# Output projection of the first batch placed inside the state-space loop, and u computed a chunk ahead

## The chip, the cores and the metric

The kernel runs on one core of one Trainium2 chip. The metric is the device time of one execution in microseconds (us); lower is better. The engines of the core work side by side and wait for one another by semaphores: TensorE (PE in the profile, its weight loads PEld), VectorE (DVE), ScalarE (ACT), GpSimd (POOL) and SyncE (SP), which here only issues DMA transfers.

## What is computed

One decoder block for a batch of 2 sequences with 512 rows and 1024 columns: a state-space mixer, a quantised product with a context matrix, and a quantised feed-forward part, each added to x. The change touches the mixer and the start of the second part. The mixer of one batch row (D = 2048, N = 16):

```python
proj = hidden_states @ W_in.T
u, gate = jnp.split(proj, 2, axis=-1)
u = jax.nn.silu(causal_conv(u, conv_w) + conv_b)          # 4 taps
dt, Bm, Cm = jnp.split(u @ Wx.T, [R, R + N], axis=-1)     # each then _rmsnorm
delta = jax.nn.softplus(dt @ Wdt.T + dt_bias)
def step(state, xs):                                      # over the 512 rows
    state = jnp.exp(d_t[..., None] * A) * state + (d_t * u_t)[..., None] * B_t[:, None, :]
    y_t = jnp.einsum('bdn,bn->bd', state, C_t)
y = (ys + u * D_param) * jax.nn.silu(gate)
return y @ W_out.T                                        # the output projection
```

(`causal_conv` stands for the reference's convolution call.)

## The kernel before, in words

The program is three functions one after the other, each of which ends when all its engines are done: `mixer`, `attend` (the context product) and `feed_forward`.

**The loop of the mixer.** The 2048 channels are cut in 16 chunks of 128, the chunks in 4 groups of 4 (GD = 4). With two batches that makes 8 groups G = 0 to 7; 0 to 3 are the first batch, 4 to 7 (GROUPS = 4 and up) the second. In each group the 16 states are 16 steps n, so there are 128 steps s = 16 G + n. In a step ScalarE computes four decays (`decay`), GpSimd four products with B (`times_b`), and VectorE runs four scans over time (`scan`, j = 0 to 3), one for each chunk. TensorE turns the scanned states of the step (`turn_state`, 16 transposes in four parts t = 0 to 3), which it can start when the fourth scan is done, so its step n lies beside step n+1 of VectorE. VectorE adds three of the four turned parts to `acc` (`add_states`) between its next scans, ScalarE and GpSimd the fourth. A VectorE instruction of step n+1 waits for TensorE if TensorE is late by more than a scan.

**Work laid beside the steps.** Every engine's program is written out by hand in one order, and functions of G and n say what stands in which step: on TensorE, between the parts t, the products of the second batch's u (`u_part`, 8 products of 128x512 in f32 for a chunk, during G = 0 to 3), those of the gate of each group (`gate_part`, 32 for a group, range given by `gate_range`), the product that gives dt, B and C (`ssm_product`), `dt_product`, the way back of y (`turn_y`, in n = 0 to 3 of the next group) and the output projection (`wout_part`: 2 products for each of 16 chunks c of a tile of 128 rows, weights through `p_ring`). ScalarE copies the gate out of PSUM (`gate_copy`), applies silu to it at the end of n = 0 of the next group (`silu_gate`: table load, silu over 128x2048, table load), starts the convolution of a finished chunk of u (`conv_first`), whose other three taps are VectorE's (`conv_rest`). The PSUM banks are shared: `bank_u` and `bank_s` hold u, the gate or the projection by turns.

**The output projection.** Its input y is known only after a group's last step, goes to memory (`yT_dram`) and comes back turned. There are 8 tiles of 128 rows, 4 for each batch. Tiles 0 to 2 are done beside groups 5 to 7 (WOUT_BESIDE = 3, 32 products each), tile 3 after the last step (`wout_last`: half of its chunks before the last `turn_y`, half behind it). The second batch's tiles 4 to 7 are done in `attend` (`project`), beside its stages.

**`attend`.** STAGES is a pipeline over the 8 tiles: in stage i VectorE adds the projection to x for tile i (`stage_a`), codes tile i-1 (`stage_b`), finishes tile i-2 (`stage_c`) and tile i-3 (`stage_d`); TensorE first does the share of `project` that BESIDE gives to the stage, then turns tile i-1's codes, and multiplies them with the context (`cross`). `cross(i)` waits until `stage_c` of the tile before has read the banks. Tiles under FIRST take their projection from memory (`attn_dram`), the others from `bank_o`.

## Time and profile before

| What | Value |
|---|---|
| runs without profile | 1631.77 us median of 3 (1631.59 to 1633.46) |
| profiled execution | 1635.13 us, its span 1633.3 us |
| mean granted TensorE clock | 0.950 |
| busy over the span | PE 1386.8 us (85%), DVE 1318.5 (81%), ACT 932.5 (57%), POOL 930.4 (57%) |
| scans of the loop | first at 181.7 us, last ends at 1133.5 us |
| `attend` | first instruction at 1181.1 us; `feed_forward`'s first product at 1378.2 us |

All times below are of the profiled execution. A window row of the trace gives, for each engine, its busy time in a stretch; where the busy time of one engine fills the stretch, that engine is the candidate for the bound, and the waits named in square brackets at an instruction say who was waited for.

### The profile page before, as it was taken

To read this page: it belongs to the slowest core of one execution; us is meant where nothing else is said; L and a number is where in the kernel's file an instruction comes from. 1 tells how busy PE (TensorE), PEld (TensorE's weight loads), DVE (VectorE), ACT (ScalarE), POOL (GpSimd) and SP (SyncE) were. 2 spreads that over 40 slices of the span, in tenths; PEclk is the share of its full clock that TensorE was granted. 3 is DMA by queue.
4 is the path that set the end of the run, shared out by engine and by line. 5 is a ranking of instruction groups with operands and counts; after the bars stand their busy time and mean duration, and the time that the engine had idled before them with its cause. 6 is when DMAs were issued, how large, how long until landed. Compare 5 with 4: busy or idle time off the path is not lost. (4 is left out here: it accounts for less than half of the span.)

```text
span 1633.3 us, 17931 instructions
## 1 busy us (share of the span) xinstructions
PE 1386.8 (85%) x5550; PEld 724.3 (44%) x5576; DVE 1318.5 (81%) x1641; ACT 932.5 (57%) x1375; POOL 930.4 (57%) x767
## 2 busy tenths in 40 slices
PE   6998677788888887768898898888899985999798
PEld 3443243444444453444454554544444442444443
DVE  6586899999999889999999999898068465777684
ACT  1212467768767756877778778765143222567570
POOL 0000497898898868899989999896101000334200
PEclk9999798999999998987999999999999996999899
DMA  8598243453452432344574782772482104679404
GB/s 281 173 348 303 71 142 110 153 168 110 147 163 102 164 106 98 112 146 149 209 247 143 258 277 98 273 225 114 172 330 78 52 26 134 126 186 204 99 11 169
DMA packets 155468, 264.38 MB, mean 162 GB/s; under 512 B 76560, under 2 KB 94096, under 8 KB 149552
## 3 DMA queue, kind: packets, MB, share of 16 engines
q1 hardware_dynamic: 151056, 236.27, 44.7%
q10 hardware_dynamic: 4320, 27.00, 4.6%
q8 instruction: 43, 0.70, 0.2%
q14 instruction: 49, 0.40, 0.1%
HBM read 207.60 MB, written 38.60 MB: 151 GB/s over the span
## 5 line engine op out<-in xcount | busy, mean ns | idle before, releaser
L1144 DVE TENSOR_TENSOR_SCAN hbuf<-decay,hbuf 128x512 f32<-128x512 f32 x502 | 598.2, 1211 | 21.0 <-ACT decay L823 20.6
L823 ACT ACTIVATE decay<-delta,chan_sb 128x512 f32<-128x512 f32 x502 | 343.8, 687 | 226.5 <-DVE hbuf L1144 223.7
L629 PE MATMUL turn<-ident,hbuf 128*128 128x128 f32 x2048 | 327.1, 289 | 165.5 <-DVE hbuf L1144 139.8
L629 PEld LDWEIGHTS turn<-ident,hbuf 128*128 128x128 f32 x2048 | 252.5, 148 | 423.2 <-DVE hbuf L1144 217.9
L1158 DVE SCALAR_TENSOR_TENSOR acc<-turn,pn,acc 128x512 f32<-128x512 f32 x360 | 262.9, 730 | 25.5 <-PE turn L629 24.3
L978 POOL TENSOR_TENSOR hbuf<-wout,sx 128x512 f32<-128x512 f32 x172 | 213.5, 1272 | 15.0 <-DVE wout L1131 15.0
L978 POOL TENSOR_TENSOR hbuf<-du,sx 128x512 f32<-128x512 f32 x172 | 213.3, 1276 | 0.0
L999 POOL TENSOR_TENSOR acc<-acc,part 128x512 f32<-128x512 f32 x120 | 153.0, 1275 | 21.9 <-ACT part L833 21.9
L1847 PE MATMUL bank<-codes,wout 128*128 128x512 bf16 (+1 forms) x690 | 153.3, 382 | 1.7 <-PEq L1261 1.0
L611 PE MATMUL bank_g<-wout,codes 128*128 128x512 f32 x256 | 135.6, 616 | 0.0
L541 PE MATMUL bank_u<-wout 128*128 128x512 f32 x224 | 112.4, 621 | 3.4 <-DMA wout<-in_wu 2.5
L1551 POOL TENSOR_TENSOR rstd<-rstd,mhalf 128x1 f32<-128x1 f32 x16 | 12.9, 808 | 176.2 <-DVE rstd L1590 176.2
L1847 PEld LDWEIGHTS bank<-codes,wout 128*128 128x128 bf16 (+1 forms) x704 | 69.5, 99 | 85.3 <-issue 4.2
L978 POOL TENSOR_TENSOR hbuf<-du,b_more 128x512 f32<-128x512 f32 x84 | 104.6, 1278 | 0.0
L978 POOL TENSOR_TENSOR hbuf<-wout,b_more 128x512 f32<-128x512 f32 x84 | 104.4, 1275 | 0.0
L541 PE MATMUL bank_s<-wout 128*128 128x512 f32 x208 | 102.3, 607 | 0.0
L611 PE MATMUL bank_s<-wout,codes 128*128 128x512 f32 x192 | 98.3, 594 | 0.0
L1022 POOL TENSOR_TENSOR rs<-rs,mhalf 128x12 f32<-128x12 f32 x2 | 4.5, 2275 | 144.6 <-DVE rs L1107 144.6
L833 ACT ACTIVATE part<-turn,pn 128x512 f32<-128x512 f32 x120 | 80.5, 671 | 7.2 <-PE turn L629 7.1
L1006 POOL TENSOR_TENSOR y_out<-y_out,gbuf 128x512 f32<-128x512 f32 x32 | 40.8, 1274 | 69.8 <-ACT y_out L848 69.8
L1969 POOL TENSOR_TENSOR hid<-gs,wout 128x512 f32<-128x512 f32 (+1 forms) x29 | 37.0, 1275 | 70.4 <-DVE wout L2005 68.4
L765 ACT ACTIVATE wout<-wout,rnd,row_scales 128x512 f32<-128x512 f32 (+1 forms) x88 | 70.4, 800 | 0.0
(219 smaller groups left out, 2130.8 us busy)
## 6 DMA issues: line engine op xcount, KB each, us to landing
wout<-in_woutT SPq DMA_DIRECT2D x48, 512.0 KB, 4.8
sx<-bt_scratch SPq DMA_DIRECT2D x86, 256.0 KB, 3.7
codes<-in_wg SPq DMA_DIRECT2D x8, 2048.0 KB, 9.9
ubuf<-u_scratch SPq DMA_DIRECT2D x16, 1024.0 KB, 7.0
wout<-in_w_gate SPq DMA_DIRECT2D x26, 512.0 KB, 4.9
wout<-in_w_up SPq DMA_DIRECT2D x26, 512.0 KB, 4.9
raw_d<-in_w_down ACTq DMA_DIRECT2D x8, 1376.0 KB, 7.2
b_more<-bt_scratch SPq DMA_DIRECT2D x42, 256.0 KB, 3.6
```

The costliest lines, as they stand in the source:

```text
L541: last = pe.matmul(u_bank(i)[:, :], w_ring[:, i % 2, k * P:k * P + P], xT[:, k, b * L:b * L + L], start=(k == 0), stop=(k == KC - 1))
L611: mm = pe.matmul(gate_bank(G, j)[:, :], wg_buf[:, k, j * P:j * P + P], xT[:, k, b * L:b * L + L], start=(k == 0), stop=(k == KC - 1))
L629: last = pe.transpose(turn[t % 2][:, j * P:j * P + P], hbuf[:, s % 4, j, t * P:t * P + P], ident[:, :])
L765: act.activation(v, v, ACT.Identity, bias=rnd[0:n, 0:1], scale=keep.iw[0:n, u % 2, c:c + 1])\
L823: act.activation(decay_place(q), delta[:, G % 2, j, :], ACT.Exp, scale=a_col(GD * (G % GROUPS) + j, n)).then_inc(dA_done, 1)
L833: act.activation(part[:, k % 2, :], turn[ZT % 2][:, :], ACT.Copy, scale=pn[:, G // GROUPS, ZT, c:c + 1]).then_inc(part_done, 1)
L978: pool.tensor_tensor(hbuf[:, s % 4, j, :], du[G % 2][:, j, :], b_row[s % 3], ALU.mult).then_inc(dbu_done, 1)
L999: pool.tensor_tensor(a, a, part[:, k % 2, :], ALU.add).then_inc(part_added, 1)
L1006: pool.tensor_tensor(y, y, gbuf[:, j, :], ALU.mult).then_inc(y_done, 1)
L1144: dve.tensor_tensor_scan(h, decay_place(q), h, 0.0, ALU.mult, ALU.add).then_inc(scan_done, 1)
L1158: dve.scalar_tensor_tensor(a, state, pn[:, G // GROUPS, t, c:c + 1], a, ALU.mult, ALU.add)\
L1847: last = pe.matmul(banks(c, b)[0:r, :], wT[:, c % WT, m, k, 0:r], keep.codes[:, k, b * L:b * L + L], start=(k == 0), stop=(k == KC - 1))
```

## The change

It moves work between places in the written order, and changes no arithmetic. The core of the diff:

```diff
-        WOUT_BESIDE = GROUPS - 1
+        WOUT_BESIDE = GROUPS
+        P_FIRST = (2, 3, 2, 3, 3, 3)
+        def p_products(s):
+            G, n = s // N, s % N
+            if G == GROUPS and 9 <= n < 9 + len(P_FIRST):
+                return P_FIRST[n - 9]
+            return 2 if G > GROUPS and n < KC else 0
...
+        def u_products(s):
+            G, n = s // N, s % N
+            if G >= GROUPS:
+                return 0
+            if G == GROUPS - 1:
+                return 6 if n < 4 else 0
+            return 4 if n < (8 if G == 0 else 6) or n >= 14 else 0
...
         def gate_range(G, n):
-            lo, per = (9, 3) if G == 0 else (5, 3) if G == GROUPS - 1 else (8, 4)
+            lo, per = (6, 4) if 1 <= G < GROUPS else (1, 4) if G == GROUPS else (8, 4)
...
         def gate_copies(G, n):
-            at = (-1, -1, 14, 16) if G == 0 else (9, 12, 14, 16) if G == GROUPS - 1 else (12, 14, 15, 16)
+            at = (-1, -1, 12, 14) if G == 0 else (9, 12, 14, 15) if G == GROUPS - 1 else (10, 12, 14, 15) if G < GROUPS else (4, 6, 8, 10) if G == GROUPS else (12, 14, 15, 16)
...
+        SSM_AT = (10, 12)
...
-            return 5 if G == GROUPS - 1 else 9 if G < GROUPS - 1 else None
+            return 5 if G == GROUPS - 1 else (9, 7, 7)[G] if G < GROUPS - 1 else None
...
-            return q % GD == 2 and (n == 1 and G >= 1 or n == 10 and G < GROUPS - 1)
+            if j == 3:
+                return n == 1 and G == GROUPS
+            return j == 2 and (n == 1 and G >= 1 or G < GROUPS - 1 and n == silu_u_step(G) + 1)
...
-            wout_last(KC, DC)
+            wout_last(KC, 3 * GD)
             for j in range(GD):
                 turn_y(NG - 1, j)
             wout_last(0, KC)
+            wout_last(3 * GD, DC)
...
+                    if not early_decay(GD * s + 3):
+                        decay(s, 3)
                     if n == 0 and G >= 1:
                         for j in gate_copies(G - 1, N):
                             gate_copy(G - 1, j)
-                    decay(s, 3)
...
-                    if b == 1 and g >= 1 and n == 9:
-                        wout_copy(g - 1)
+                    if G > GROUPS and n == 9:
+                        wout_copy(g)
+                    if G == GROUPS + 1 and n == 0:
+                        wout_copy(0)
...
-    FIRST = TT
+    FIRST = TT + 1
-    BESIDE = [[((TT, TT + 1), DC // 4 * i, DC // 4 * (i + 1))] for i in range(4)]
-    BESIDE += [[((TT + 2,), 0, 8)], [((TT + 2,), 8, DC), ((TT + 3,), 0, 2)], [((TT + 3,), 2, 9)], [((TT + 3,), 9, DC)]]
+    BESIDE = [[((FIRST,), 0, 8)], [((FIRST,), 8, DC)]] + [[((FIRST + 1,), 4 * i, 4 * i + 4)] for i in range(4)]
+    BESIDE[5] += [((FIRST + 2,), 0, 2)]
+    BESIDE += [[((FIRST + 2,), 2, 9)], [((FIRST + 2,), 9, DC)]]
```

In words. All four tiles of the first batch are projected in the loop: tile 0 beside steps 9 to 14 of group 4, tiles 1 to 3 beside groups 5 to 7; group 4's gate moves up to steps 1 to 8 to make room. Tile 4, the second batch's first, takes the place behind the last step: its chunks 8 to 11 before the last `turn_y`, chunks 0 to 7 behind it, and last chunks 12 to 15, which come from the last group and are stored and loaded in between (`load_yT_last(1)`). `attend` projects three tiles (5, 6, 7). The second batch's u is computed a chunk ahead: one chunk of the next group already in steps 14 and 15, so that its `conv_first` stands at the end of step 0 of the next group. `ssm_product` of groups 0 to 2 is split in two halves, in steps 10 and 12, and gets a bank of its own (`ssm_bank`); its sum `add_ssm` moves from step 15 to 14. The gates of groups 1 to 3 end in step 13 and their last copy moves from step 0 of the next group to step 15 (14 for group 0). In groups 6 and 7 it stays in step 0, but behind `decay(s, 3)`. One semaphore (`ms_done`) goes and `yT_keep` comes.

TensorE's order in `attend`, stages 2 and 3 (a row is a run of equal instructions; `bank_o` is `project`, `bank_t` the turning of codes, `bank_p<-ctx_q,codeT` is `cross`). Before:

```order
L1418 MATMUL bank_o<-wout,codes 128x512 x16
L1433 MATMUL bank_t<-identb,code 128x128 x8
L1450 MATMUL bank_b<-ones,codeT 128x1 x8
L1461 MATMUL bank_p<-ctx_q,codeT 128x512 x16
L1418 MATMUL bank_o<-wout,codes 128x512 x16
L1433 MATMUL bank_t<-identb,code 128x128 x8
```

And now:

```order
L1483 MATMUL bank_o<-wout,yT 128x512 x8
L1498 MATMUL bank_t<-identb,code 128x128 x8
L1515 MATMUL bank_b<-ones,codeT 128x1 x8
L1526 MATMUL bank_p<-ctx_q,codeT 128x512 x16
L1483 MATMUL bank_o<-wout,yT 128x512 x8
L1498 MATMUL bank_t<-identb,code 128x128 x8
```

The share of `project` ahead of each `cross` is halved in stages 2, 3 and 4, and in stage 5 it goes from 20 products to 12; in stages 0, 1, 6 and 7 it is as long as before. (A product of the order is two instructions in the trace.)

ScalarE's order at the head of a group (steps 0 and 1 of group 2; `gbuf<-bank_s` is the gate copy, `gbuf<-gbuf` the silu, `wout<-bank_u` is `conv_first`). Before:

```order
L765 ACTIVATE wout<-wout,rnd,row_scales 128x512
L854 ACTIVATE gbuf<-bank_s 128x512
L823 ACTIVATE decay<-delta,chan_sb 128x512 x2
L833 ACTIVATE part<-turn,pn 128x512
L823 ACTIVATE decay<-delta,chan_sb 128x512
L823 ACTIVATE bank_g<-delta,chan_sb 128x512
L858 ACT_TABLE_LOAD
L858 ACTIVATE gbuf<-gbuf 128x2048
L859 ACT_TABLE_LOAD
L823 ACTIVATE decay<-delta,chan_sb 128x512 x3
```

And now:

```order
L818 ACTIVATE wout<-wout,rnd,row_scales 128x512
L878 ACTIVATE decay<-delta,chan_sb 128x512 x2
L888 ACTIVATE part<-turn,pn 128x512
L878 ACTIVATE decay<-delta,chan_sb 128x512
L878 ACTIVATE bank_g<-delta,chan_sb 128x512
L913 ACT_TABLE_LOAD
L913 ACTIVATE gbuf<-gbuf 128x2048
L914 ACT_TABLE_LOAD
L797 ACTIVATE wout<-bank_u,chan_sb 128x512
L801 DMA wout<-in_wu 128x1024
L878 ACTIVATE decay<-delta,chan_sb 128x512 x3
```

The gate copy ahead of the decays is gone from here, and a `conv_first` stands between the silu and the next decays. VectorE's `conv_rest` for it is in step 1, after the second scan.

TensorE's order in steps 10 and 11 of group 4 (`turn` is `turn_state`; the other rows are the gate before and `wout_part` now). Before:

```order
L588 MATMUL bank_m<-ssm,wdt_sb 128x512
L629 MATMUL turn<-ident,hbuf 128x128 x4
L611 MATMUL bank_s<-wout,codes 128x512
L629 MATMUL turn<-ident,hbuf 128x128 x4
L611 MATMUL bank_s<-wout,codes 128x512
```

And now:

```order
L634 MATMUL bank_m<-ssm,wdt_sb 128x512
L675 MATMUL turn<-ident,hbuf 128x128 x8
L706 MATMUL bank_u<-wout 128x512
L706 MATMUL bank_s<-wout 128x512
L675 MATMUL turn<-ident,hbuf 128x128 x4
L706 MATMUL bank_u<-wout 128x512
L706 MATMUL bank_s<-wout 128x512
L675 MATMUL turn<-ident,hbuf 128x128 x4
```

The first row is step 9's `dt_product`; the parts t of a step that have no product between them run together (x8). Step 10 holds six products of the projection (three chunks, the third behind the last row here) where it held four of the gate; step 11 holds four.

## Rows read from the trace of the kernel before

Columns of a window row: from:to, length, busy us (and instructions) of PE, PEld, DVE, ACT and POOL, granted TensorE clock (share of full speed), share of the DMA engines, GB/s.

**Rows 1.** Windows: groups 1, 3, 4, 5, the mixer's end, `attend`:

```profile
307.40:428.60 121.20, 101.95 (x432) 57.55 (x432) 116.27 (x131) 92.34 (x140) 107.61 (x88) 0.96 0.43 145
...
551.40:690.50 139.10, 111.48 (x452) 61.55 (x452) 124.25 (x143) 94.23 (x142) 107.42 (x87) 0.93 0.35 119
690.50:801.20 110.70, 85.43 (x364) 51.43 (x364) 106.66 (x118) 85.68 (x133) 106.71 (x88) 0.85 0.42 138
801.20:912.80 111.60, 99.16 (x432) 55.31 (x432) 106.77 (x118) 86.92 (x136) 106.21 (x87) 1.00 0.63 215
...
1133.50:1181.10 47.60, 40.91 (x128) 20.39 (x128) 2.25 (x3) 10.40 (x15) 6.54 (x6) 0.99 0.45 166
1181.10:1343.00 161.90, 152.83 (x553) 71.57 (x561) 100.13 (x175) 49.28 (x54) 10.71 (x17) 0.98 0.34 124
```

**Rows 2.** The same view for one stage of `attend`:

```profile
1259.10:1279.30 20.20, 18.99 (x76) 9.04 (x75) 12.51 (x23) 4.73 (x6) 1.10 (x2) 1.00 0.15 52
```

**Rows 3.** TensorE in `attend`, in order of time (start us, us):

```profile
1236.80 3.40 PE L1461 MATMUL bank_p<-ctx_q,codeT 128*128 128x512 bf16 x15
...
1255.92 3.40 PE L1461 MATMUL bank_p<-ctx_q,codeT 128*128 128x512 bf16 x15
...
1260.06 13.97 PE L1418 MATMUL bank_o<-wout,yT 128*128 128x512 f32 x32
...
1276.03 1.67 PE L1461 MATMUL bank_p<-ctx_q,codeT 128*128 128x512 bf16 x7
```

**Rows 4.** VectorE in `attend`, in order of time:

```profile
1231.12 0.75 DVE L1633 SCALAR_TENSOR_TENSOR xr<-fix,sc,xr 128x512 f32<-128x512 f32 x1
...
1238.18 0.69 DVE L1577 TENSOR_SCALAR ctx_raw<-ctx_raw 128x1024 f32<-128x1024 f32 x1 [4.55 <-ACT ctx_raw L1496]
...
1243.50 0.81 DVE L1610 TENSOR_SCALAR xn<-xr,mv,rstd 128x1024 f32<-128x1024 f32 x1
...
1253.07 0.75 DVE L1633 SCALAR_TENSOR_TENSOR xr<-fix,sc,xr 128x512 f32<-128x512 f32 x1
...
1268.12 0.75 DVE L1633 SCALAR_TENSOR_TENSOR xr<-fix,sc,xr 128x512 f32<-128x512 f32 x1
```

**Rows 5.** ScalarE, then VectorE, at step 0 of group 2:

```profile
434.19 0.60 ACT L854 ACTIVATE gbuf<-bank_s 128x512 f32<-128x512 f32 x1 [2.72 <-PE bank_s L611]
...
442.50 1.30 ACT L823 ACTIVATE decay<-delta,chan_sb 128x512 f32<-128x512 f32 x2
...
435.40 2.34 DVE L1144 TENSOR_TENSOR_SCAN hbuf<-decay,hbuf 128x512 f32<-128x512 f32 x2 [1.41 <-ACT decay L823]
```

**Rows 6.** VectorE: a `conv_rest`, and the wait in step 15 behind `ssm_product`:

```profile
379.47 2.31 DVE L1077 SCALAR_TENSOR_TENSOR wout<-bank_s,chan_sb,wout 128x511 f32<-128x511 f32 x3
...
422.67 0.75 DVE L1158 SCALAR_TENSOR_TENSOR acc<-turn,pn,acc 128x512 f32<-128x512 f32 x1 [1.23 <-PE turn L629]
```

**Rows 7.** Windows: group 1 step 1; group 3 steps 1-6, step 4; group 4 step 6:

```profile
313.87:322.33 8.46, 8.32 (x34) 5.18 (x35) 7.38 (x9) 7.60 (x8) 7.48 (x7) 0.82 0.53 216
...
559.30:620.20 60.90, 54.72 (x214) 31.29 (x214) 49.35 (x57) 37.59 (x51) 41.11 (x34) 0.92 0.42 145
...
590.40:600.80 10.40, 10.40 (x43) 5.93 (x42) 8.83 (x12) 5.92 (x9) 7.46 (x7) 1.00 0.16 50
...
733.00:739.40 6.40, 5.65 (x18) 3.31 (x18) 6.40 (x8) 4.74 (x7) 6.40 (x7) 0.53 0.60 199
```

**Rows 8.** TensorE in a step that follows an idle time, group 1:

```profile
368.13 1.12 PE L629 MATMUL turn<-ident,hbuf 128*128 128x128 f32 x4 [3.25 <-DVE hbuf L1144]
...
372.43 0.60 PE L629 MATMUL turn<-ident,hbuf 128*128 128x128 f32 x4
...
375.12 1.12 PE L588 MATMUL bank_m<-ssm,wdt_sb 64*128 64x512 f32 x2
```

**Rows 9.** The mixer's end: GpSimd's last gated y, and SyncE's issues:

```profile
1164.23 1.26 POOL L1006 TENSOR_TENSOR y_out<-y_out,gbuf 128x512 f32<-128x512 f32 x1 [1.44 <-ACT y_out L848]
...
1167.85 0.81 SPq L501 DMA_DIRECT2D codes<-yT_scratch  x2
```

More of the change, by code:

```diff
@@ L218, in u_count @@
             return Gu + 1 + (Gu >= GROUPS - 1)
-        RELU_STEP = 9
+        MS_STEP = (7, 21)
+        RELU_STEP = 10
         def unit_rows(u):
@@ L712, in _ @@
                         turn_y(G - 1, n)
-                    if G < GROUPS - 1 and n == 13 or G == GROUPS - 1 and n == 5:
+                    if G < GROUPS - 1 and n in SSM_AT:
+                        ssm_product(GROUPS + g, 2 * SSM_AT.index(n), 2 * SSM_AT.index(n) + 2)
+                    if G == GROUPS - 1 and n == 5:
                         ssm_product(GROUPS + g)
@@ L937, in _ @@
                         decay(s + 1, 1)
-                        if early_decay(GD * (s + 1) + 2):
-                            decay(s + 1, 2)
+                        for j in range(2, GD):
+                            if early_decay(GD * (s + 1) + j):
+                                decay(s + 1, j)
                     if paired:
@@ L1384, in _ @@
             load_attn(2)
+            load_yT(1)
             load_yT(2)
-            load_yT(3)
             load_x(3)
```

195 lines of the change are left out of this document (114 added, 81 removed).

## The prediction

> **What bounds the kernel now.** I read the windows by stretch first. In the loop VectorE is the full engine: 116.3 of 121.2 us in group 1, 106.7 of 110.7 in group 4 [rows 1]. A step in which nothing goes wrong takes 6.4 us, all of it VectorE (last of [rows 7]). So work laid beside a step on TensorE is free as long as TensorE is done in time, and a step gets longer either by VectorE's own work (a `conv_rest` is 2.31 us, 2.23 with the overlap [rows 6]) or by a wait of VectorE. In `attend` it is the other way round: TensorE is busy 152.8 of 161.9 us, VectorE 100.1 [rows 1], and in one stage of 20.2 us TensorE has 19.0 and VectorE 12.5 [rows 2]. Of such a stage `project` is 13.97 us for 32 instructions [rows 3], so 0.44 us for one and 0.87 us for a product of the order.
>
> The Trainium skill speaks against me here. It says (Trainium Kernel Development and Optimization, Performance Expectations) that matmul busy time is a bad metric, because matmuls are pipelined; if the 152.8 us were only overlapping ends, nothing would come of taking products out. But the 32 instructions stand in 13.97 us from first start to last end, 0.44 us apart at full clock, with no wait named. So I count the trace's spacing; by the skill's doubt this part would be worth 0.
>
> **attend: minus 20.** The change takes one tile of four out: 16 instructions (8 products) in each of stages 2 to 5, 16 x 0.437 = 7.0 us a stage, 28 in all. I follow which wait comes last then.
> Stage 2: `cross` starts at 1236.80 [rows 3]. TensorE would be there at 1229.8, but it must wait for `stage_c` of the tile before, which ends at 1231.12 + 0.75 = 1231.9 [rows 4]. Gain 4.9.
> Stage 3: VectorE waited for ScalarE's context pieces until 1238.18 [rows 4], and ScalarE for TensorE. Now it is free of stage 2's work at 1233.6, so the pieces (5.3 us, 1238.18 to 1243.50) end at about 1239.0, 4.5 earlier. From 1243.50 to the end of `stage_c` at 1253.07 + 0.75 are 10.3 us of VectorE, so the next `cross` can start at 1249.3 instead of 1255.92. Gain so far 6.6.
> Stage 4: VectorE needed 1268.87 - 1253.82 = 15.1 us to the next end of `stage_c`, 2.2 of it waits for ScalarE that goes with TensorE: 12.9, so 1262.2. TensorE's way is 20.1 (1276.03 - 1255.92) - 7.0 = 13.1, so 1262.4. Gain 13.6.
> Stage 5: 12 products left, TensorE bound again: another 7.0, 20.6. Stages 6 and 7 are as long as before and TensorE bound, and the tail behind them moves along. I take **20.3**. Bounds: 28 if VectorE gives way, 13 if stages 4 and 5 each lose half.
>
> **The mixer's end: 0.** TensorE has 40.9 of 47.6 us there [rows 1], 32 products before and now. What is new is that the last 4 chunks wait for y of group 7 to be stored and loaded. 4 chunks fewer stand ahead of the last `turn_y`, so all of y is 8 x 0.87 = 6.9 us earlier: GpSimd ends at 1165.5 - 6.9 = 1158.6, the stores have landed at 1167.85 - 6.9 = 1161.0 [rows 9]. The load of 256 KB then has the 6.9 + 2.3 us until TensorE has done chunks 0 to 7. A transfer would have to take over 9 us to be seen.
>
> **Step 0 of a group: minus 7.7.** ScalarE's gate copy waits for TensorE until 434.19 and stands ahead of `decay(s, 3)`, so the fourth scan waits 1.41 [rows 5]; groups 2, 3, 5, 6 and 7 have this 1.41, group 4 has 1.05. The copy moves to step 15 for groups 2 to 5: 1.5 + 1.5 + 1.15 + 1.5 with the overlap that the wait breaks. In groups 6 and 7 the copy stays but behind the decay: it then delays the next decay by some 0.5, gain 1.0 each.
>
> **A conv at step 1: plus 2.3, and a cold TensorE: plus 3.** Step 1 takes 8.46 us, since ScalarE is in the table loads and the silu (first of [rows 7]). One would hope that the conv of the chunk ahead fills this hole. It doesn't: `conv_first` stands behind the silu, where the decays resume at 442.50, 6.0 us after the step's first scan at 436.5 [rows 5]. With its 0.7 us the conv can begin at 6.7 and VectorE sits in front of it from 4.4; then 2.2 of conv, scan, add, scan: the step ends at 11.9 instead of 8.46. That is 3.4 for a conv that cost 2.2 elsewhere: +1.2 in each of groups 1 and 2 (group 3 below). While VectorE waits TensorE is idle for about 4 us. After 3.25 idle, two sets of transposes and two products take 372.43 - 368.13 = 4.3 us instead of 375.12 - 372.43 = 2.7 [rows 8], at half clock. TensorE's step 1 holds 4 products and `turn_y`, some 7.1 us, 8.7 with this; VectorE's step 2 lasts 6.4 and forgives 0.6 more, so step 3 waits 1.5: +3.0 for two groups. Bounds for both terms together: 0 and 9.
>
> **Groups 0 to 2, rest: minus 5.** `ssm_product` in one piece (8 instructions, 3.5 us) makes step 15 wait 1.23 in groups 1 and 2 and 0.86 in group 0 [rows 6]. Halves of 1.7 beside 4 gate products make 7.1 us of TensorE, within what a step forgives: -3.4 (the broken overlap included; -1 if the halves wait as well). With silu of u at step 7, step 8, which waited for a cold TensorE, and step 10, which waited for the silu, become one: -0.9 twice.
>
> **Group 3: minus 4.** Steps 1 to 4 carried 8 products of u, and TensorE fills them: 10.40 of 10.40 us at full clock (third of [rows 7]). Steps 1 to 6 took 60.9 us (second of [rows 7]). With 6 products such a step is 10.4 - 1.7 = 8.7, the same as VectorE with a conv (6.4 + 2.2). Step 1 becomes 11.9, step 2 6.4, step 3 8.7 + 3.4 of lateness from step 2's 8.7 + 1.6 cold, then 8.8, 8.8 and the silu's 9.4: 57.4. -3.5 here; its step 0 is counted above. The wait of chunk 15 for the conv of chunk 13 falls in this lateness. With what the earlier end of the gates spares I take **-4**.
>
> **Group 4: 0.** 32 products more, 27.8 us, on a TensorE with 85.4 of 110.7 busy [rows 1]. Step 1: `decay(s, 3)` now goes ahead of the silu, -1.1. Waits in steps 5 to 9 cost 2.2 (110.7 less 16 x 6.43, 4 x 0.6 of `delta_add`, and 3.2 in steps 0 and 1), and they come from TensorE at half clock: 0.53 in step 6, where it has only transposes [rows 7]. The gate at steps 1 to 8 keeps the clock up: -2.2. Against it: six products and the transposes are 7.1 to 7.4 us, over 6.43, in steps 10, 12, 13 and 14, a third of which VectorE feels, +1; the first chunk waits at step 9 for a gate copy that ScalarE makes in step 10, +1.2; steps 14 and 15 of group 3 have only transposes now, so the group starts at half clock, +1.
> The Trainium skill (TensorE: Matmul & The Clock Gate, Part 4: PE-mode transpose) says that PE-mode transposes do not count as busy for the clock; the rows agree (0.53 with only transposes, 1.00 in group 5, where products are mixed in [rows 1]). If products so mixed did not count either, the rule would cost this change dearly, which is the rival below.
> Groups 5 to 7 hold what they held. `load_yT(1)` can only start when tile 0 is done, at step 15; if it is late, step 1 has slack.
>
> **Sum.** -20.3 (attend), 0, -7.7, +5.3, -5.2, -4, -0.1: -32.0. Against the profiled execution of 1635.1 (span 1633.3) that is 1603.1; that execution is 3.4 above the median without profile, so against 1631.77: **1599.8**.
>
> **Rivals.**
> (a) The chain in `attend` does not go at TensorE's pace once a tile is out: ScalarE's in-order copies and `stage_c` take turns, and stages 2 to 5 give 8 to 10 instead of 20. For it: VectorE's 12.9 and TensorE's 13.1 leave nothing over, and stage 3 is already lost. Against: ScalarE has 4.7 us in a stage of 20 [rows 2]. 1611.
> (b) The loop gives nothing: the conv behind the silu costs its upper bound 9, and the ssm halves wait too. 1611 to 1613. For it: TensorE's slack in group 1 is only 19 us [rows 1].
> (c) More than I count: `conv_first` costs little, group 4 gains 3: 1593.
> (d) Slower: mixed with transposes the projection's products are not enough to keep the clock, and group 4 runs at half clock throughout. Then its 64 products take 1.74 instead of 0.87, the transposes 3.8 instead of 1.9 a step, the group some 180 us instead of 110: 1670. It decides once seven of its 16 steps run so (4 to 5 us each against the 32). Against it: group 5 has the same mix at clock 1.00 [rows 1].
> (e) No change: products in `attend` are hidden anyway, and the loop breaks even.
>
> **How the numbers follow.** Forecast 0.70, (a) 0.10, (b) 0.11, (c) 0.06, (d) 0.02, (e) 0.01. The range reaches to (c) below and to (a) above, 1592 to 1611. A measurement of this kernel tells 0.2%, 3.3 us, from no change: faster in all cases but (d) and (e), 0.97, same 0.01, slower 0.02.
>
> **What would show it.** Right: `cross` to `cross` some 13 us in stages 3 and 4, `attend` 20 us shorter; the fourth scan of step 0 waits no more in groups 2 to 5; step 1 of groups 1 to 3 takes 11 to 12 us with VectorE's wait in front of `conv_rest`; steps 2 to 5 of group 3 under 9.5 us but one; the last 4 chunks of tile 4 start without a wait. Wrong: TensorE's clock at half in steps 9 to 14 of group 4, VectorE waiting there for TensorE by more than 1 us a step, or stages of 16 us and more in `attend`.

## The result, and the profile after

| | before | after |
|---|---|---|
| runs | 1632.62 us median of 4 | 1621.62 us median of 4 (1621.10 to 1627.92) |
| ratio | | 0.9932, 95% interval 0.9904 to 0.9961 |
| profiled execution, its span | 1635.13, 1633.3 | 1627.92, 1626.0 |
| start to the first scan | 181.7 | 178.6 |
| the loop, first scan to last | 951.8 | 957.1 |
| last scan to the first product of `attend` | 47.7 | 47.5 |
| `attend`, first product to the first of feed-forward | 197.0 | 178.8 |
| feed-forward to the end | 255.1 | 264.0 |

About 11 us faster where 32 were forecast; the range (1592 to 1611) doesn't hold it. The first and the last part of the table are untouched by the change and vary from one execution to the next: the start took 177.7 to 181.7 us and feed-forward 254.2 to 267.4 in the twelve traces of this case. The three parts between give 5.3 - 0.2 - 18.2 = -13.1. So `attend` did nearly what was forecast (-20.3) and the loop did not: +5.3 where the steps add up to -11.7.

The windows of after that answer to [rows 1]: groups 1, 3, 4 and 5, the mixer's end, `attend`.

```profile
306.00:428.10 122.10, 103.77 (x441) 58.16 (x440) 116.05 (x131) 92.83 (x141) 106.49 (x87) 0.97 0.42 139
550.60:688.00 137.40, 109.27 (x440) 61.94 (x440) 124.08 (x142) 94.05 (x143) 108.49 (x87) 0.89 0.39 133
688.00:801.60 113.60, 103.78 (x431) 60.20 (x432) 107.11 (x118) 85.76 (x134) 108.10 (x89) 0.92 0.58 189
801.60:916.80 115.20, 99.89 (x426) 56.10 (x424) 106.87 (x118) 87.45 (x137) 104.95 (x86) 0.96 0.68 235
1135.60:1183.10 47.50, 40.92 (x128) 20.39 (x128) 2.27 (x4) 10.40 (x15) 6.57 (x6) 1.00 0.43 149
1183.10:1327.20 144.10, 126.48 (x489) 59.30 (x497) 99.78 (x174) 49.32 (x54) 12.89 (x17) 0.96 0.39 143
```

VectorE's busy time is what it was (107.1 us in group 4 for 106.7, 106.9 in group 5 for 106.8): what the loop lost is waits of VectorE. In `attend` TensorE has 26.4 us less work and the stretch is 17.8 shorter.

Group by group, from the first scan of one to the first scan of the next, with my forecast put together from the prediction's terms, and the control, which is a second trace of the same kernel:

| group | before | after | change | forecast | control |
|---|---|---|---|---|---|
| 0 | 125.74 | 127.42 | +1.7 | -0.9 | 127.80 |
| 1 | 121.16 | 122.15 | +1.0 | +0.6 | 122.09 |
| 2 | 122.80 | 122.36 | -0.4 | -1.0 | 122.37 |
| 3 | 139.06 | 137.39 | -1.7 | -5.5 | 137.33 |
| 4 | 110.76 | 113.57 | +2.8 | -1.3 | 113.56 |
| 5 | 111.60 | 115.23 | +3.6 | -1.5 | 113.36 |
| 6 | 111.38 | 110.92 | -0.5 | -1.0 | 110.77 |
| 7 | 109.28 | 108.02 | -1.3 | -1.0 | 108.00 |

Groups 3, 4 and 5 miss by 13 us together. I went there step by step (a step runs from its first scan to the next step's) and looked at what VectorE waits for. Four places of after, in order of time; each row has start, length, engine, line, operation, and in brackets the idle time ahead of it and who ended it.

```profile
315.14 1.91 ACT L913 ACTIVATE gbuf<-gbuf 128x2048 f32<-128x2048 f32 x1
...
318.36 0.78 ACT L797 ACTIVATE wout<-bank_u,chan_sb 128x512 f32<-128x512 f32 x1
...
319.17 2.32 DVE L1136 SCALAR_TENSOR_TENSOR wout<-bank_u,chan_sb,wout 128x511 f32<-128x511 f32 x3 [3.16 <-ACT wout L797]
...
631.15 1.06 PE L675 MATMUL turn<-ident,hbuf 128*128 128x128 f32 x4 [3.46 <-DVE hbuf L1204]
632.01 1.92 PE L657 MATMUL bank_u<-wout,codes 128*128 128x512 f32 x2
...
634.81 0.75 DVE L1218 SCALAR_TENSOR_TENSOR acc<-turn,pn,acc 128x512 f32<-128x512 f32 x1 [0.68 <-PE turn L675]
...
759.78 0.58 ACT L909 ACTIVATE gbuf<-bank_s 128x512 f32<-128x512 f32 x1
...
760.57 1.66 PE L706 MATMUL bank_u<-wout 128*128 128x512 f32 x2 [3.19 <-issue]
...
764.69 0.75 DVE L1218 SCALAR_TENSOR_TENSOR acc<-turn,pn,acc 128x512 f32<-128x512 f32 x1 [3.20 <-PE turn L675]
...
803.35 0.60 SPq L447 DMA_DIRECT2D wout<-yT_scratch  x1
...
812.80 2.04 PE L706 MATMUL bank_u<-wout 128*128 128x512 f32 x2 [2.81 <-issue]
...
817.44 0.75 DVE L1215 TENSOR_SCALAR acc<-turn,pn 128x512 f32<-128x512 f32 x1 [4.47 <-PE turn L675]
...
822.63 0.75 DVE L1218 SCALAR_TENSOR_TENSOR acc<-turn,pn,acc 128x512 f32<-128x512 f32 x1 [1.53 <-PE turn L675]
```

- **315 to 319, step 1 of group 1** (groups 2 and 3 alike): `conv_first` stands behind the silu and its table load, VectorE waits 3.16. The step takes 12.55, forecast 11.9.
- **631 to 635, steps 8 and 9 of group 3**: TensorE comes back from 3.46 idle at half clock (a product 1.92 instead of 1.02), with four gate products to do where it had three. VectorE waits here (0.68) and twice more (0.68 and 1.62); steps 9 to 11 take 12.77, 7.42 and 8.15 instead of 11.55, 6.63 and 7.73.
- **760 to 765, step 10 of group 4**: the first product of tile 0 starts 0.2 after the gate copy's end at 760.36. TensorE stood 3.19 for it, with the step's transposes behind it, and VectorE stood 3.20 for those.
- **803 to 823, steps 0 to 2 of group 5**: `load_yT(1)` is issued at 803.35, 1.9 after the group's first scan; the first product of tile 1 starts 9.45 later, at half clock, again ahead of the transposes. VectorE waits 4.47 and 1.53.

The last two are one pattern: an instruction of TensorE that waits for something else, with `turn_state` behind it in the order, which VectorE needs.

`attend` after, TensorE in order of time, answering to [rows 3]; start, length:

```profile
1234.27 3.40 PE L1526 MATMUL bank_p<-ctx_q,codeT 128*128 128x512 bf16 x15 [1.11 <-DVE xr L1698]
...
1251.37 1.01 PE L1526 MATMUL bank_p<-ctx_q,codeT 128*128 128x512 bf16 x2 [3.30 <-DVE xr L1698]
1252.60 4.61 PE L1526 MATMUL bank_p<-ctx_q,codeT 128*128 128x512 bf16 x13 [0.22 <-issue]
...
1257.77 7.03 PE L1483 MATMUL bank_o<-wout,yT 128*128 128x512 f32 x16
...
1267.12 3.40 PE L1526 MATMUL bank_p<-ctx_q,codeT 128*128 128x512 bf16 x15 [0.41 <-DVE xr L1698]
```

`project` is 7.03 us a stage where it was 13.97: the 7.0 of the forecast. In stage 3 TensorE waits 3.30 for VectorE and then does `cross` at half clock (5.84 from first start to last end instead of 3.40). The `cross` of stage 2 stands behind 1.11 of idle time here and keeps full clock; in the control it took 5.09 behind the same 1.11.

### The profile page after: what moved, and what is told of

The parts are those of the page before. It is cut to its first block and busy times, and to the rows that moved or that the text cites. A ratio compares the mean times of both kernels' runs of the same rounds, so it can differ in the third digit from the quotient of the medians.

```text
span 1626.0 us, 17958 instructions
## 1 busy us (share of the span) xinstructions
PE 1383.0 (85%) x5550; PEld 722.4 (44%) x5576; DVE 1318.0 (81%) x1640; ACT 934.2 (57%) x1377; POOL 932.4 (57%) x767
## 5 line engine op out<-in xcount | busy, mean ns | idle before, releaser
L583 PE MATMUL bank_u<-wout 128*128 128x512 f32 x224 | 112.4, 617 | 2.5 <-DMA wout<-in_wu 1.7
L888 ACT ACTIVATE part<-turn,pn 128x512 f32<-128x512 f32 x120 | 80.5, 671 | 13.4 <-PE turn L675 13.3
L706 PE MATMUL bank_u<-wout 128*128 128x512 f32 x128 | 67.7, 611 | 6.0 <-issue 6.0
```

The lines of the kernel that those rows point to most:

```text
L583: last = pe.matmul(u_bank(i)[:, :], w_ring[:, i % 2, k * P:k * P + P], xT[:, k, b * L:b * L + L], start=(k == 0), stop=(k == KC - 1))
L706: last = pe.matmul(bank[:, :], yT_view[c], p_ring[q % 4][:, half * 512:half * 512 + 512], start=(c == 0), stop=(c == DC - 1))
L888: act.activation(part[:, k % 2, :], turn[ZT % 2][:, :], ACT.Copy, scale=pn[:, G // GROUPS, ZT, c:c + 1]).then_inc(part_done, 1)
```

## The experiments

Each edit is measured against the kernel before. The intervals reach 0.2 to 0.4% to either side, 3 to 6 us, as wide as most of the effects; so a kernel's time says whether the whole adds up, and the verdict on a step is read from its trace against the control's. "Loop" is first scan to last scan.

| run | median us | ratio to before, 95% | loop |
|---|---|---|---|
| control | 1622.02 | 0.9919 (0.9895 to 0.9942) | 955.27 |
| conv_first ahead | 1609.91 | 0.9836 (0.9813 to 0.9860) | 944.24 |
| tile 1 later | 1617.47 | 0.9895 (0.9872 to 0.9918) | 955.10 |
| load_wg later | 1624.94 | 0.9927 (0.9903 to 0.9951) | 959.49 |
| group 4's gate earlier | 1617.25 | 0.9897 (0.9875 to 0.9919) | 954.40 |
| attend cut otherwise | 1619.94 | 0.9913 (0.9888 to 0.9937) | 957.06 |
| ssm in one piece | 1625.77 | 0.9953 (0.9934 to 0.9972) | 961.63 |
| group 3's gate thinner | 1621.66 | 0.9913 (0.9888 to 0.9939) | 953.59 |
| before, decay first | 1629.31 | 0.9967 (0.9938 to 0.9996) | 949.63 |
| four together | 1600.57 | 0.9791 (0.9754 to 0.9828) | 937.38 |

**The control**, the changed kernel unedited.

> The changed kernel again, unedited, beside the kernel before, as the measure for the other runs of this chip. Expected: 0.9932 of the kernel before within 0.002, step 1 of the sixth group (group 5) 11.7 us and of groups 1 to 3 12.5 us as in its first trace. If the 11.7 us were an accident of one execution, it would be near 8.5 here.

0.9919: the first ratio again within its error. Step 1 of group 5 took 10.81 and step 2 7.24 (11.66 and 8.09 in the first trace), so the loss there is no accident of one execution, but its size varies by 1.7 us. `attend` took 177.6. By this trace the change is +3.5 in the loop and -19.4 in `attend`.

**conv_first ahead of the silu.**

```diff
+                    c = u_chunk_ready(s)
+                    if n == 0 and c is not None:
+                        conv_first(DC + c)
+                        load_w_after(DC + c)
                     if n == 0 and G >= 1:
                         silu_gate(G - 1)
                     quant(s, 1)
-                    c = u_chunk_ready(s)
-                    if c is not None:
+                    if c is not None and n > 0:
```

> The changed kernel, with the first part of the conv at step 0 of groups 1 to 3 issued by ScalarE ahead of the silu of the gate and not behind it. Theory: step 1 of these groups takes 12.5 us because VectorE stands 3.15 us in front of conv_rest for a ScalarE that is still in the silu, and step 3 is then late by 0.9 to 2.2 because TensorE comes back cold. Then step 1 falls to about 9.2 us (its 8.5 plus what of the conv's 2.2 doesn't fit in the hole), VectorE's wait there is gone, step 3 loses its wait, and the kernel gets 10 to 12 us faster than the changed one: about 1610 us, 0.986 of before. Rival: ScalarE itself is what is full there, and the conv ahead of the silu only pushes the decays of step 1 back by its 0.7 us and the wait moves from conv_rest to the scans; then the gain is under 3 us. Second rival: the cold TensorE is not due to that wait, and step 3 keeps its 1 to 2 us while step 1 gets shorter: 7 us.

Step 1 of group 1 in its trace, ScalarE and VectorE:

```profile
315.68 0.76 ACT L797 ACTIVATE wout<-bank_u,chan_sb 128x512 f32<-128x512 f32 x1
...
317.85 2.31 DVE L1139 SCALAR_TENSOR_TENSOR wout<-bank_u,chan_sb,wout 128x511 f32<-128x511 f32 x3
...
320.97 1.30 ACT L878 ACTIVATE decay<-delta,chan_sb 128x512 f32<-128x512 f32 x2
```

`conv_rest` has no wait in front of it any more. It fills the time in which VectorE would have stood for the decays, which resume 6.7 us into the step (6.0 in the kernel before, where no conv was there; 6.6 in the control). Step 1 takes 9.30 in groups 1 to 3 (12.54 in the control) and step 3 is down to 8.66 in groups 1 and 2 (9.64 and 9.81) and 9.97 in group 3 (10.97). Loop -11.0, ratio -0.0083: the first theory in place and size; the two rivals are out. The wait of step 3 in groups 1 and 2 went together with VectorE's wait in step 1, as the theory of TensorE's cold start (at half clock behind idle time) has it. Steps 1 to 3 of the three groups give 13.7, and steps 6 and 7 of groups 1 and 2 take 2.4 of it back.

**Tile 1 a step later.**

```diff
+            if G == GROUPS + 1:
+                return (0, 2, 2, 2, 2, 2, 3, 3)[n] if n < KC else 0
```

> The changed kernel, with no products of the output projection in step 0 of group 5 and 2,2,2,2,2,3,3 in steps 1 to 7, where it has 2 in each of steps 0 to 7. Theory: load_yT(1) can only be issued at the end of group 4, lands some 9 us later, and TensorE stands in front of the first product with turn_y behind it, on which VectorE's add waits (4.5 us in step 1 and 1.5 in step 2). Then step 1 is 7.3 to 8.5 us instead of 11.7, step 2 6.5 to 7.2 instead of 8.1, nothing is lost in steps 6 and 7 (3 products there beside transposes, at most 0.5 each), and the kernel is 4 to 5 us faster than the changed one, 0.990 to 0.991 of before. Rival: the wait is TensorE's clock after its idle stretch, not the load; then step 1 keeps 10 us or more.

Issue of the load, and the first product of tile 1:

```profile
802.75 0.60 SPq L449 DMA_DIRECT2D wout<-yT_scratch  x1
...
816.72 1.02 PE L708 MATMUL bank_u<-wout 128*128 128x512 f32 x2
```

The product starts without a wait and at full clock, steps 1 and 2 take 8.46 and 6.45: -3.1 against the control, -4.8 against the first trace. So the wait was the load. But the three products in steps 6 and 7 were no "0.5 at most": steps 8 and 9 take 7.50 and 8.75 instead of 7.03 and 6.46, with a wait of 2.18 for TensorE. Group 5 as a whole is 112.97 for 113.36. The control is the shortest of the seven traces in which this group stands as in the changed kernel (113.36 to 115.30, steps 1 and 2 together 18.1 to 19.8 us, 14.9 here), so the edit is worth 0.4 to 2.3 us. The place was right; 2.8 us of the gain were given back in steps 8 and 9 by a TensorE that was behind.

**The gate's weights two steps later.**

```diff
-                    if n == 1 and G >= 1 and G != GROUPS:
+                    if n == (3 if G == GROUPS + 1 else 1) and G >= 1 and G != GROUPS:
                         load_wg(G)
```

> The changed kernel, with the load of the gate's weights (2 MB) for group 5 issued two steps later, behind load_yT(1) and the other loads of step 1. Two theories of the late load. If it is late because 2 MB share the DMA engines with it, its time from issue to landing falls from about 9 us to 4 or 5, step 1 of group 5 is 8 to 9 us instead of 11.7, and the kernel gains 3 us. If it is late because it starts late (at the end of group 4, when tile 0 is done) and its own transfer takes those 9 us, step 1 stays at 11 us or more and the kernel is unchanged within 1 us.

```profile
806.22 0.60 SPq L447 DMA_DIRECT2D wout<-yT_scratch  x1
...
815.69 2.04 PE L706 MATMUL bank_u<-wout 128*128 128x512 f32 x2 [2.82 <-issue]
```

9.47 us from issue to the product, as in after (9.45) and the control (9.43): the 2 MB beside it are not what makes it late. Steps 1 and 2 took 11.68 and 8.08, as in the first trace; step 4 got 2.5 longer: ScalarE's copy of a turned y waits 4.05 us there for the store of the y before it (1.62 in after), and that store was issued at 838.05, with the 2 MB, now issued at 832.36, under way beside it. Below, the DMA view of this kernel from 806 to 816 (busy tenths and GB/s of the engines in slices of 0.25 us, the sum, the loads with size and us from issue to landing), then that of the kernel before from 798 to 810 (slices of 0.3), where the load is issued at 799.90, 1.3 ahead of the group's first scan.

```profile
DMA  7989979899899999999999999999999999999966
GB/s 311 459 360 492 410 328 492 360 426 459 344 492 377 426 426 377 426 393 402 418 369 418 393 377 401 401 385 393 385 393 393 410 410 410 442 434 369 385 270 262
...
q1 hardware_dynamic: 1510, 3.97, 100.5%
...
wout<-yT_scratch SPq DMA_DIRECT2D x1, 1024.0 KB, 9.4
```

```profile
DMA  9820000045655578999999999999999999999979
...
wout<-yT_scratch SPq DMA_DIRECT2D x1, 1024.0 KB, 6.3
```

So the load starts 3.2 us later within the group than before and takes 3.1 longer. It starts later because it is written to wait for the last product of tile 0, which ends at 805.27 here. That it takes longer because the 16 DMA engines are full I infer from this view: 3.97 MB pass in the 10 us, 1 MB of it this load, while before they stood idle when it was issued. What fills them without the 2 MB was issued just ahead, above all three pieces of 512 KB for `load_p` (800.99 to 805.6 here) and u's 1 MB (799.25), and 1 MB right behind. No run took any of these away, so this part of the cause is argued and not shown. The Trainium skill (DMA: Bandwidth & Descriptors, Where 436 GB/s comes from) gives 435 GB/s as the ceiling of the SBUF ports, and the 397 GB/s of this trace stay under it. It puts transfers between HBM and SBUF, which these are, at about 358 a core; the trace lies above that, and the measurement decides.

**Group 4's gate a step earlier.**

```diff
+            if G == GROUPS:
+                at = [0, 0, 4, 8, 12, 17, 22, 27, 32]
+                return at[min(n, 8)], at[min(n + 1, 8)]
...
-(4, 6, 8, 10) if G == GROUPS
+(4, 6, 8, 9) if G == GROUPS
```

> The changed kernel, with group 4's gate products given out as 4,4,4,5,5,5,5 in steps 1 to 7 (4 in each of steps 1 to 8 before) and its last gate copy made in step 9, not 10. Theory: step 10 of group 4 takes 10.35 us because the projection's first chunk stands on TensorE behind ScalarE's gate copy, with the transposes for VectorE's add behind it (wait 3.2). Then step 10 falls to 7.1 or less and steps 11 and 12 to 7.0, at the price of at most 0.3 us in each of steps 4 to 7: 3 to 4 us in all, about 0.990 of before. Rival: it is TensorE's work of that step (products and transposes) and not the copy; then step 10 stays above 9 us.

Step 10 takes 7.03 (10.34 in the control), step 11 7.22 (7.34), step 7 6.99 (6.43): group 4 is 2.9 shorter. It was the copy. But group 5 took 115.30 for 113.36:

```profile
802.62 0.60 SPq L450 DMA_DIRECT2D wout<-yT_scratch  x1
...
812.32 2.04 PE L709 MATMUL bank_u<-wout 128*128 128x512 f32 x2 [2.72 <-issue]
```

Its first scan is at 799.92, so the load is issued 2.7 behind it (after: 1.9; control: 1.9), 9.70 to the product. Whether the wait for tile 1 took part of what the copy's wait gave back is not shown: the first trace of the changed kernel had 115.23 without the edit.

**attend cut otherwise.**

```diff
-        + [[((FIRST + 1,), 4 * i, 4 * i + 4)] for i in range(4)]
+        + [[((FIRST + 1,), lo, hi)] for lo, hi in ((0, 5), (5, 11), (11, 15), (15, DC))]
```

> The changed kernel, with tile 6 of the second batch's projection cut as 5, 6, 4 and 1 products over attend's stages 2 to 5, not 4 in each. Theory: in stages 2 and 3 TensorE stands idle for 1.1 to 3.3 us in front of cross, and after the longest of these it does cross at half clock (5.84 us instead of 2.9); a product of the order put there fills the gap and keeps the clock. Then cross to cross in stage 3 is 13 us where it was 15.7 to 17.1, the stages from 2 to 5 together are 4 to 6 us shorter, and the kernel 0.990 of before. Rival: VectorE and ScalarE set the pace of stages 2 and 3 whatever TensorE does, the clock included; then attend gains less than 1.5 us (only what stage 5 is spared).

```profile
1252.92 3.61 PE L1527 MATMUL bank_p<-ctx_q,codeT 128*128 128x512 bf16 x16 [1.47 <-DVE xr L1699]
...
1266.23 3.61 PE L1527 MATMUL bank_p<-ctx_q,codeT 128*128 128x512 bf16 x16 [0.19 <-DVE xr L1699]
...
1279.55 6.40 PE L1508 MATMUL bank_p<-ctx_q,ones 128*128 128x512 bf16 x16 [3.38 <-DVE xr L1699]
```

The idle time in front of the `cross` at 1252.92 fell from 3.23 (control) to 1.47 and it kept full clock; from it to the next are 13.3 us for 15.2. But from the `cross` before it there are 17.3 for 17.1, since VectorE has no gap between the two in either trace, and the idle time came back in stage 5 (3.38, then 16 instructions at half clock in 6.40): that stage is 21.3 for 19.9. `attend` took 178.0 for 177.6. The rival holds: VectorE sets stages 2 to 5 together now, and a product moved among them moves TensorE's idle time with it. (The 2.9 us that the expectation gives for a `cross` at full clock is 3.40 in the rows.)

**ssm_product in one piece.**

```diff
-                    if G < GROUPS - 1 and n in SSM_AT:
-                        ssm_product(GROUPS + g, 2 * SSM_AT.index(n), 2 * SSM_AT.index(n) + 2)
+                    if G < GROUPS - 1 and n == 12:
+                        ssm_product(GROUPS + g)
```

> The changed kernel, with ssm_product of groups 0 to 2 in one piece at step 12 instead of halves in steps 10 and 12. The prediction counted 3.4 us for taking the piece apart. If that is what the halves are good for, the one piece makes VectorE wait about 1.2 us in step 13 of each of groups 0 to 2, and the kernel gets 2.5 to 3.5 us slower than the changed one. If the gain is only that the product no longer stands at step 14 beside the next u's products, place and not size, it is the same within 1 us. In group 0, where the halves make steps 12 and 14 of 7.25 and 7.6 us, one piece may even be better by 0.5.

Group 1, the product on TensorE and the wait behind it:

```profile
413.65 3.60 PE L608 MATMUL bank_u<-wout,wx_buf 128*96 128x512 f32 x8
...
417.73 0.75 DVE L1218 SCALAR_TENSOR_TENSOR acc<-turn,pn,acc 128x512 f32<-128x512 f32 x1 [1.83 <-PE turn L675]
```

The wait came in step 14 (414.71 to 424.25), not 13, and was 1.83. Group 1 is 1.6 longer than the control's, group 2 3.7 (1.5 of it here, the rest in waits for TensorE at other steps), the ratio 0.0034 higher, with intervals that just overlap: by the trace the halves do work, and it is size, not only place. Group 0 took 127.15 for 127.80 and 127.42: nothing lost by one piece there.

**Group 3's gate thinner.**

```diff
+            if G == GROUPS - 1:
+                at = [0, 4, 7, 10, 13, 17, 21, 25, 29, 32]
+                return at[min(max(n - 6, 0), 9)], at[min(max(n - 5, 0), 9)]
```

> The changed kernel, with group 3's gate products given out as 4,3,3,3,4,4,4,4,3 in steps 6 to 14 instead of 4 in each of 6 to 13. Theory: steps 9 to 11 of group 3 (12.77, 7.42 and 8.15 us; 11.55, 6.63 and 7.73 before the change) are long by 2.4 because four gate products, not three, stand beside the norm and the turns on a TensorE that comes back cold from 3.5 us idle. Then these three steps give back 1.5 to 2.4 us and nothing is lost in 12 to 14: 0.991 of before. Rival: what makes them long is the order of ScalarE's and VectorE's work for the norm (MS at step 7), not TensorE's products; then steps 9 to 11 stay within 0.5 us.

Steps 9 to 11 take 11.54, 6.63 and 8.71: 26.9 for 28.3 in the control, just under the theory's 1.5 to 2.4, and nothing lost in 12 to 14. In two traces with the gate unthinned ("tile 1 later", "ssm in one piece") the three steps take 27.8, so the edit is worth 0.9 to 1.4 there. The other half of what it brings came where I hadn't looked. Windows of group 3's step 15 and group 4's steps 0 to 2, first of the control, then of this kernel (last but two: granted clock):

```profile
684.09:690.52 6.43, 3.42 (x16) 2.28 (x16) 6.43 (x8) 5.63 (x10) 6.43 (x6) 0.58 0.98 415
690.52:697.16 6.64, 4.19 (x16) 3.00 (x16) 6.55 (x9) 4.64 (x7) 6.64 (x7) 0.50 0.71 221
697.16:704.45 7.29, 6.47 (x21) 4.27 (x22) 7.19 (x10) 7.12 (x8) 7.29 (x7) 0.50 0.40 142
704.45:711.63 7.18, 7.18 (x33) 4.71 (x33) 6.56 (x8) 4.51 (x7) 4.55 (x4) 0.92 0.10 37
```

```profile
680.35:686.78 6.43, 4.79 (x22) 2.51 (x22) 6.43 (x9) 5.03 (x10) 6.43 (x6) 1.00 0.11 23
686.78:693.24 6.46, 2.46 (x16) 1.68 (x16) 6.46 (x9) 5.02 (x8) 6.46 (x6) 0.99 0.90 364
693.24:700.53 7.29, 5.81 (x29) 4.33 (x30) 7.19 (x10) 7.12 (x8) 7.10 (x7) 0.77 0.96 337
700.53:706.99 6.46, 6.46 (x32) 3.74 (x30) 6.46 (x9) 4.51 (x7) 4.99 (x5) 1.00 0.39 128
```

In the control TensorE has nothing but the 16 transposes in step 15 and step 0, runs them at 0.58 and 0.50, the 1.2 GHz level, and comes into step 1 at 0.50; 33 instructions then fill all of step 2 and VectorE waits in steps 2 to 5. With three more gate products, written in step 14 and run in step 15 (22 instructions in the first row for 16), step 0 is granted 0.99, step 1 0.77, and steps 2 and 3 take 6.46 and 6.43 instead of 7.18 and 6.95. Group 4 is 1.5 shorter, group 3 1.4. The loop is only 1.7 shorter than the control's, since group 5 took 114.96, within what it takes without an edit.

**The kernel before, with decay first.**

```diff
-                    if n == 0 and G >= 1:
-                        for j in gate_copies(G - 1, N):
-                            gate_copy(G - 1, j)
...
                     decay(s, 3)
+                    if n == 0 and G >= 1:
+                        for j in gate_copies(G - 1, N):
+                            gate_copy(G - 1, j)
```

> The kernel before, with one piece of the change alone: in step 0 of groups 1 to 7 ScalarE makes decay(s, 3) ahead of the gate copy of the group before, not behind it. Theory (the prediction's -1.0 where the copy stays in step 0): the wait of 1.4 us in front of the fourth scan goes, the next decay is delayed by some 0.5, so step 0 of groups 2, 3, 5, 6 and 7 is 0.8 to 1.1 us shorter each, group 4's 0.6 to 0.9, and the kernel is 4 to 6 us faster than before, 0.997. Rival: the delayed decays of step 1, where ScalarE has the silu, hand it back there (0.3 us of this is seen in groups 6 and 7 of the changed kernel, whose step 1 went from 8.47 to 8.81): then under 2 us are left. It also gives a second trace of group 0 as before: 125.7 us there, or up to 127.8 if what group 0 lost is the execution's and not the change's.

VectorE at the end of step 0 and in step 1 of group 2:

```profile
437.70 1.22 DVE L1144 TENSOR_TENSOR_SCAN hbuf<-decay,hbuf 128x512 f32<-128x512 f32 x1 [0.28 <-ACT decay L823]
...
444.73 1.22 DVE L1144 TENSOR_TENSOR_SCAN hbuf<-decay,hbuf 128x512 f32<-128x512 f32 x1 [1.62 <-ACT decay L823]
```

Step 0 falls from 7.93 to 6.79, and step 1 rises from 8.46 to 8.81: net 0.8, in groups 4 to 7 too; in group 3 the two steps give 1.9. Together 5.8, so the theory holds and the rival, under 2 us, is out; the time is 0.9967 of before, -5.4 with an interval of 4.8. The loop of this trace is only 2.2 shorter, because groups 0 and 1 took 127.32 and 124.15 for 125.74 and 121.16, with waits for TensorE at steps that the edit doesn't touch. So group 0 of the kernel before can itself take 127.3, and the +1.7 of the changed kernel there is inside what executions vary.

**Four edits together.**

> The changed kernel with four edits that were measured apart: conv_first ahead of the silu in step 0, group 5's products 0,2,2,2,2,2,3,3, group 4's gate 4,4,4,5,5,5,5 with its last copy in step 9, group 3's gate 4,3,3,3,4,4,4,4,3. Summed from their traces against the control's: -11.0 (steps 1 to 3 and on of groups 1 to 3), -2.9 (group 4), -2.9 (groups 3 and 4 after the lighter gate), and -0.4 to -2.3 in group 5: the loop in 936 to 940 us where the control has 955.3, and the kernel in 1601 to 1605 us, 0.980. Rival: what an edit gives is taken by the next wait, above all in steps 0 and 1 of group 5, where tile 1's operand comes from memory when it comes; then 1606 to 1610.

Windows of this kernel, groups 1, 3, 4, 5 and `attend` up to feed-forward:

```profile
306.60:427.90 121.30, 105.34 (x441) 58.85 (x440) 116.22 (x131) 92.94 (x141) 106.46 (x87) 0.96 0.41 140
...
547.10:676.60 129.50, 106.53 (x440) 60.03 (x440) 122.99 (x143) 93.51 (x142) 108.57 (x88) 0.92 0.37 119
676.60:785.70 109.10, 99.73 (x430) 57.54 (x431) 106.72 (x118) 85.87 (x134) 107.40 (x88) 0.97 0.67 222
785.70:897.80 112.10, 98.07 (x427) 55.49 (x425) 107.07 (x119) 87.52 (x138) 107.59 (x89) 0.98 0.70 245
...
1164.30:1342.20 177.90, 139.65 (x561) 66.42 (x562) 121.14 (x211) 60.05 (x68) 15.78 (x20) 0.90 0.38 130
```

1600.57 us, 0.9791 of before; the loop 937.4, inside the 936 to 940 summed from the single traces, and the time just under the 1601 to 1605 expected. So the edits add up, and the rival (1606 to 1610) is out. Group 3 is 129.5 for 137.3, group 4 109.2 for 113.6, and `attend` is where it was. It is 1.3% below the control's ratio (0.9791 against 0.9919, intervals apart).

## Why the prediction was wrong

The three middle parts were forecast to give 32.0 us and gave 13.1 (16.1 in the control). The 18.9 between are 5.1 in group 5, 4.1 in group 4, 3.8 in group 3, 2.6 in group 0, 2.1 in `attend` and 1.2 in the other groups. The steps of the prediction that failed are, in this order: that a late `load_yT(1)` costs nothing, the price of the first chunk's wait for the gate copy, that an earlier end of the gates spares something in group 3, and TensorE's pace in stage 4 of `attend`. The loop gave nothing, as in rival (b), but not by (b)'s way: the conv behind the silu cost 5.7 for the 5.3 forecast, not 9, and the ssm halves saved 0.9 in each of groups 1 and 2.

**attend, -20.3: nearly right** (-18.2; -19.4 in the control; 177.6 to 179.5 us in the ten traces with three tiles in it). Counted from the first `cross`, stage 3's gain was forecast at 6.6 and is 6.6; stage 4's at 13.6 and is 10.9; stage 5's at 20.6 and is 17.8. So the step that was mis-sized is stage 4: I gave TensorE's way there 20.1 - 7.0, at full clock, while it begins at half clock behind 3.30 of idle time, 2.4 us dearer. Undoing that alone gives nothing (experiment "attend cut otherwise"), since VectorE, which I counted as level with TensorE, holds the stages together. The instructions' spacing in the rows was the right price, 7.0 us a stage. The Trainium skill (Trainium Kernel Development and Optimization, Performance Expectations) calls matmul busy time a bad metric for how close a kernel is to roofline. It doesn't say what taking products out is worth; the 0 that the prediction drew from it was my reading, and the trace doesn't bear it out.

**The mixer's end, 0: right** (47.7 to 47.5; the last four chunks have no wait in front).

**Step 0, -7.7: right.** -1.5 in groups 2 and 3, -0.9 in 4, -1.2 in 5, -1.1 in 6 and 7, -7.4 in all. In groups 6 and 7 step 1 pays 0.34 of it back, the delayed decay for which the prediction took off 0.5: net 0.8 each for the 1.0 forecast, and the experiment on the kernel before shows the same 0.8 alone.

**A conv at step 1, +2.3 and +3.0: right.** Step 1 is 12.55, not 11.9: the conv begins 6.8 into the step, where I had 6.7, but two scans and two adds follow it in the step and not "scan, add, scan", one add of 0.65 more. VectorE's waits in step 3 of groups 1 and 2 are 0.87 and 1.12 where I said 1.5. Steps 1 to 3 are 5.0 and 5.2 us longer in these groups, 2.2 of it the conv that stood elsewhere before, so the two terms together are +5.7 for +5.3. What I didn't ask is whether the order itself is needed: put ahead of the silu, the same conv costs 0.8 in the step and not 4.1, and the loop is 11 us shorter.

**Groups 0 to 2, rest, -5.2: right in two groups of three.** Silu of u at step 7 is there (steps 8 to 10 of group 1 take 8.71, 6.43 and 7.03 for 7.95, 8.66 and 8.72: 3.2 less, 2.2 of it the conv that went to step 1). The ssm halves (steps 11 to 15) gave 0.9 in each of groups 1 and 2 for the 1.25 forecast, the halves themselves being worth 1.5 against one piece at step 12. In group 0 nothing was gained: steps 11 to 15 take 34.8 in the control and 36.6 in the first trace for 34.9. The wait of step 11 there is also in the kernel with one piece, so it is not the halves; what it is stays open.

**Group 3, -4: -0.2 without its step 0.** Steps 1 to 6, where I counted, are 57.75 for the 57.4 forecast. The step that failed is the last sentence, "With what the earlier end of the gates spares I take -4": an earlier end means four gate products a step where there were three, and in steps 9 to 11, with TensorE cold from the norm, that cost 2.4. The thinner gate gave 0.9 to 1.4 of it back. How much of the rest is the clock is open: TensorE came back at half clock from the 3.46 of idle time in step 9, and at full clock from 3.83 in the same place of the kernel before (eight transposes in 1.09, where after has four in 1.06):

```profile
636.18 1.09 PE L629 MATMUL turn<-ident,hbuf 128*128 128x128 f32 x8 [3.83 <-DVE hbuf L1144]
```

**Group 4, -0.1: +3.8 without its step 0.** Right: `decay(s, 3)` early (step 1 -1.2), the gate keeps the clock (steps 5 to 9 -1.7 for 2.2). Too small: "the first chunk waits at step 9 for a gate copy that ScalarE makes in step 10, +1.2" is 3.2, because I priced only how late the chunk is, and not that TensorE goes idle with the step's transposes behind the chunk and comes back at half clock (1.66 and 1.91 for 1.02). Taking the copy earlier gave 3.4 in steps 10 and 11. The "+1" for the start at half clock is 1.8 in steps 2 to 4, and the "+1" for six products beside the transposes is 1.6 in steps 11 to 14. The rival (d), half clock throughout, is out: in steps 9 to 14, where the projection stands, the granted clock is 1.00 except for 0.84 in step 10, and the control's is 0.92 in step 2 and 1.00 in steps 3 to 7. That a stretch with nothing but transposes is granted 0.50 and one right behind three products 0.99 is what both sets of windows show. The Trainium skill (TensorE: Matmul & The Clock Gate, Part 4: PE-mode transpose) says that transposes don't count as busy for the clock, and the rows at 0.58 and 0.50 agree.

**"Groups 5 to 7 hold what they held. `load_yT(1)` can only start when tile 0 is done, at step 15; if it is late, step 1 has slack": wrong, the largest miss, +4.8** in steps 1 and 2 of group 5 (+3.1 in the control). I saw the late start and dismissed it by VectorE's slack for ScalarE in step 1. But TensorE's first product of the tile is written in step 0, and everything VectorE needs of TensorE in step 1 stands behind it. The load's length I took for nothing: it is 9.4 us where the trace of before would have said 6.3, and from 3.2 us later in the group.

Of the signs that I named for "wrong" two are in the trace, each in one place: VectorE waits more than 1 us for TensorE in step 10 of group 4 (3.20), and stage 3 of `attend` takes 17.1. The second was badly chosen. The prediction's own chain gives stage 3 17.4 us (1231.9 to 1249.3), so neither "16 us and more" as a sign of wrong nor "some 13 us in stages 3 and 4" as a sign of right fitted it; stage 4 took 15.8 for 13.1. The sign of half clock in steps 9 to 14 is not there except behind the idle time of step 10. I looked for the danger where TensorE is full, and it was where TensorE waits.

## What to carry to other kernels

When work is put beside the bounding engine on an in-order engine, don't price only its length: list what each of its instructions waits for (a copy, a load, a buffer), and what stands behind it that the bounding engine needs; a first chunk ahead of the transposes cost 3.3 us in group 4 and 3 to 5 in group 5, while the fuller steps behind the first in group 4 cost 1.6. Price the restart too, since the engine that had waited 3 us came back at half clock in each of these places of the changed kernel (in the kernel before it once came back at full clock from 3.83). And when an operation lands in a stretch in which another engine is shut off (ScalarE in a table load), ask on which side of it the operation's first part stands: one such swap was worth 11 us, as much as the whole change.
